# LM tower on one core: the first 16 score tiles of batch 0 straight from the projected rows

## The reference

```python
base = base_embeddings[ids]; rule = token_rules[ids]
h = einsum('bsd,bsde->bse', base, rule_transform[rule])        # one 64x64 matrix per token
xn = layernorm(h)
q = einsum('btd,hrd->bhtr', xn, Q); k = einsum('bud,hrd->bhur', xn, K)
attn = softmax(einsum('bhtr,bhur->bhtu', q, k) / sqrt(64))
h = h + einsum('bhtd,hde->bte', einsum('bhtu,bud->bhtd', attn, xn), VO)
x2 = layernorm(h)
gate = x2 @ Wg + bg + bias; w = softmax of the top 2, else 0
h = h + sum over e of w[e] * (relu(x2 @ W1[e] + b1[e]) @ W2[e] + b2[e])
```

## Time and profile before

| | us |
|---|---|
| median of 3 runs | 615.68 |
| lowest, highest | 615.65, 620.51 |
| profiled execution | 619.58 |
| its span, first to last instruction | 617.5 |
| mean granted TensorE clock | 0.923 of full |

### The profile page before, as it was taken

The page is one execution under the profiler, slowest core; times in us unless marked ns, Lnnn a source line. Parts: engine busy times, 40 slices in busy tenths (PEclk is TensorE's granted clock), DMA queues, the critical chain, the costliest instruction groups (busy, mean ns, idle before and its releaser), DMA issues.

```text
span 617.5 us, 9436 instructions
## 1 busy us (share of the span) xinstructions
PE 499.3 (81%) x2732; PEld 268.7 (44%) x2732; DVE 410.7 (67%) x1003; ACT 287.2 (47%) x581; POOL 228.3 (37%) x375
## 2 busy tenths in 40 slices
PE   0066603778679896999999999999999989999985
PEld 0035501234444342445544544454454444575753
DVE  5532486645215874978869877895975776665577
ACT  0203301025545543456564565556456546547664
POOL 5664356463225300340254145122413313181542
PEclk9998755559979997999999999999999999999989
DMA  8815212733381062440440422044042200000000
GB/s 234 312 59 152 79 36 61 179 95 103 95 229 40 14 155 53 102 113 5 100 114 2 102 63 60 1 104 113 1 96 68 53 2 2 11 2 10 11 2 17
DMA packets 21791, 47.05 MB, mean 76 GB/s; under 512 B 6248, under 2 KB 11576, under 8 KB 21680
## 3 DMA queue, kind: packets, MB, share of 16 engines
q1 hardware_dynamic: 15408, 32.23, 21.5%
q0 software_dynamic: 4752, 8.20, 4.9%
q10 hardware_dynamic: 1584, 6.03, 3.0%
HBM read 9.97 MB, written 11.01 MB: 34 GB/s over the span
## 4 chain that ended last, share of the span: by engine, by line
PE 54%; DVE 19%; issue 8%; DMA 6%; POOL 6%; ACT 3%; SPq 3%; another core or an unknown queue 0%; DVEq 0%; ACTq 0%; POOLq 0%
PE bank L1274 14%; PE bank L1260 10%; PE bank L1240 7%; PE bank L1202 4%; PE bank L1224 4%; DVE mx L997 3%; POOL emb_sorted L527 2%; DMA ctxT<-in_table,ids 2%; PE bank L1196 2%; PE bank L1197 2%; DVE r_sb L1055 2%; POOL ctxT L517 2%; PE bank L1132 2%; POOL r_sb L591 2%; DMA ks<-qk_l 1%
## 5 line engine op out<-in xcount | busy, mean ns | idle before, releaser
L997 DVE TENSOR_REDUCE mx<-bank 128x1 f32<-128x512 f32 x256 | 170.5, 687 | 83.5 <-PE bank L1260 75.3
L591 POOL TENSOR_TENSOR r_sb<-r_sb 128x256 f32<-128x256 f32 x174 | 91.0, 523 | 251.8 <-DVE r_sb L1073 171.4
L671 ACT ACTIVATE prob<-bank 128x512 f32<-128x512 f32 x256 | 139.0, 597 | 58.5 <-PE bank L1240 43.0
L1260 PE MATMUL bank<-ks,qs 96*128 96x512 f32 x256 | 122.7, 487 | 14.4 <-DVE mx L997 9.7
L1274 PE MATMUL bank<-prob,xa 128*64 128x512 f32 x448 | 123.5, 630 | 0.7 <-ACT ctxT L685 0.7
L1260 PEld LDWEIGHTS bank<-ks,qs 96*128 96x128 f32 x256 | 50.9, 199 | 130.8 <-issue 109.5
L1240 PE MATMUL bank<-qs,ks 97*128 97x512 f32 x224 | 78.1, 430 | 0.0
L738 ACT ACTIVATE r_sb<-bank,stay 128x512 f32<-128x512 f32 x56 | 37.1, 687 | 44.9 <-PE bank L1197 44.6
L1240 PEld LDWEIGHTS bank<-qs,ks 97*128 97x128 f32 x224 | 38.4, 194 | 15.6 <-issue 11.1
L527 POOL DMA_INDIRECT emb_sorted<-ctxT,pos x32 | 32.0, 1001 | 22.6 <-DMA emb_sorted<-ctxT,pos 11.7
L517 POOL DMA_INDIRECT ctxT<-in_table,ids x32 | 32.4, 1011 | 21.3 <-DMA ctxT<-in_table,ids 8.6
(11 more groups left out here) (167 smaller groups left out, 659.3 us busy)
## 6 DMA issues: line engine op xcount, KB each, us to landing
qs<-qk_h SPq DMA_DIRECT2D x64, 128.0 KB
ks<-qk_h SPq DMA_DIRECT2D x56, 128.0 KB
qs<-qk_l SPq DMA_DIRECT2D x32, 128.0 KB
ks<-qk_l SPq DMA_DIRECT2D x28, 128.0 KB
emb_sorted<-front ACTq DMA_DIRECT2D x4, 608.0 KB
y_sorted<-y_out POOLq DMA_DIRECT2D x19, 128.0 KB, 2.7
e_in<-emb_sorted POOLq DMA_DIRECT2D x9, 256.0 KB, 3.2
emb_sorted<-front ACTq DMA_DIRECT2D x3, 640.0 KB
```

Of the source, the lines that this page charges most:

```text
L591: nc.gpsimd.tensor_tensor(a[:, at:at + width], src[:, 0:width], src[:, width:2 * width], ALU.add).then_inc(S["pool_chain"], 1)
L671: nc.scalar.activation(prob[:, step % NPROB, u % 2, :], bank[u % NST][:], ACT.Exp, scale=SC).then_inc(S["exp_done"], 1)
L997: V.tensor_reduce(mx[:, u // 16, u % 16:u % 16 + 1], bank[3 + n % 2][:], AX.X, ALU.max).then_inc(S["mx_done"], 1)
L1260: M(bank[3 + n % 2][:], qs[0:96, nb % 2, h, tt * 128:(tt + 1) * 128], ks[0:96, nb % 2, h, :], start=True, stop=True).then_inc(S["s_ps"], 1)
```

## The change

In the first 16 places of batch 0's 32 score tiles PE computes pairs of tiles, one of a head of stack group g = 0 and one of g = 1 (rows 0 to 31 and 32 to 63), right from qk_h and qk_l: three matmuls of 32 rows a tile, high x high, low x high, high x low, summed in a bank, the two heads' matmuls in turn. Pairs take banks 3, 4 and 0, 1 alternately. A step still has two tiles; both are issued in the place of the first. mx keeps its columns. mt(0, 0) moves from (-1, 13) to (-1, 11), norm(1) from (0, 0) to (-1, 12), xT(1) from (0, 2) to (-1, 15), proj(1) from (0, 2) and (0, 3) to (0, 0) and (0, 1), the rule entries from (-1, 14) to (0, 5) to four a step in (0, 3) to (0, 7), norm(2), xT(2) and norm(3) one step on, proj(2) all to (0, 15), `bring(0, 1)` to right behind `bring(0, 0)`. `slots` is a generator, run for (1, 3) in five pieces at (-2, 1), (-2, 2), (-2, 5), (-2, 6) and (-2, 7). Norm pieces: 4 a step in b = -1, 3 in b = 0.

```diff
@@ -243,15 +243,15 @@
                     + [("back", f, 0), ("back", f, 1), ("fold", f, J), ("fold", f, J + 1)] + [("down", f + 1, p) for p in range(NE // 2)]
                     + [("back", f, 2), ("fold", f, J + 2), ("back", f, 3), ("fold", f, J + 3)])
 
-        R_AT = [(-1, 14), (-1, 15)] + [(0, g // 3) for g in range(18)]
+        R_AT = [(0, 3 + g // 4) for g in range(20)]
 
         def x_at(nb):
 
-            return {1: (0, 2), 2: (0, 13)}.get(nb, (nb - 2, XT))
+            return {1: (-1, 15), 2: (0, 14)}.get(nb, (nb - 2, XT))
 
         def proj_at(nb):
 
-            return {1: ((0, 2), (0, 2), (0, 3), (0, 3)), 2: ((0, 14), (0, 14), (0, 15), (0, 15))}.get(
+            return {1: ((0, 0), (0, 0), (0, 1), (0, 1)), 2: ((0, 15), (0, 15), (0, 15), (0, 15))}.get(
                 nb, [(nb - 2, k) for k in PROJ])
 
         def aux_at(b, k):
@@ -275,7 +275,7 @@
                 todo.append(("rt", b - 1, 0))
             if k == GATE and 0 <= b - 2 < B:
                 todo.append(("gate", b - 2, 0))
-            if k == MT[0] and 0 <= b + 1 < B:
+            if (b, k) == (-1, 11) or k == MT[0] and 0 <= b < B - 1:
                 todo.append(("mt", b + 1, 0))
             if k in VO_STEPS and 0 <= b - 1 < B:
                 todo.append(("vo", b - 1, VO_STEPS.index(k)))
@@ -384,6 +384,11 @@
             return ctxT[:, (LAST - 1) % 2].rearrange("p q t -> p (q t)").rearrange("p (e n) -> p e n", n=HW)
 
         NST = 3
+
+        def score_bank(n):
+
+            return bank[(3 if n >= 16 or n // 2 % 2 == 0 else 0) + n % 2]
+
         es = [t.rearrange("(g p s) d -> p g (s d)", p=128, s=4) for t in emb_sorted]
         ys = [t.rearrange("(g p s) d -> g p (s d)", p=128, s=4) for t in y_sorted]
 
@@ -554,6 +559,7 @@
             for g in range(NG[0] - 4, NG[0]):
                 store_sent(pool, g)
             bring(0, 0)
+            bring(0, 1)
             pool.wait_ge(S["zeroed_1"], 16 * 4)
             place(1, range(FIRST, FIRST + 2 * QC))
             values(0)
@@ -564,8 +570,6 @@
                     if n >= NE_IN // 2:
                         pool.wait_ge(S["eT_ps"], PAIRS[n - NE_IN // 2][-1] + 1)
                     load_pair(pool, n)
-                if n == NP0 + 2:
-                    bring(0, 1)
                 for g in PAIRS[n - AHEAD] if n >= NP0 + AHEAD else ():
                     pool.wait_ge(S["y_ok"], g + 1)
                     store_group(pool, g)
@@ -824,15 +828,19 @@
                 lo = SPAN[i][0]
                 both, nth, ahead, at_in, past, gap, tile_, hi, mid, low, two = (slot_i[:, j, :] for j in range(11))
                 link(V.tensor_tensor(sel[:], oh[:, c0 - lo:c1 - lo, :], key.unsqueeze(1).to_broadcast([128, QC, NR]), ALU.mult))
+                yield
                 link(V.tensor_reduce(slot_f[:], sel[:], AX.X, ALU.add))
+                yield
                 link(V.tensor_tensor(both, slot_f[:], rank[:, c0:c1], ALU.add))
                 link(V.tensor_scalar(nth, both, SHIFT, (B * T >> SHIFT) - 1, ALU.logical_shift_right, ALU.bitwise_and))
                 link(V.tensor_scalar(ahead, both, (B * T).bit_length() - 1, None, ALU.logical_shift_right))
                 link(V.tensor_scalar(at_in, both, TS - 1, 2, ALU.bitwise_and, ALU.logical_shift_left))
+                yield
                 link(V.tensor_tensor(past, nth, ahead, ALU.add))
                 link(V.scalar_tensor_tensor(gap, past, float(NR - 1), rule_i[:, c0:c1], ALU.add, ALU.subtract))
                 link(V.scalar_tensor_tensor(past, nth, 1.0, gap, ALU.min, ALU.mult))
                 link(V.tensor_tensor(tile_, past, rule_i[:, c0:c1], ALU.add))
+                yield
                 link(V.tensor_scalar(hi, tile_, 2, None, ALU.logical_shift_right))
                 link(V.tensor_scalar(low, tile_, 3, None, ALU.bitwise_and))
                 link(V.tensor_scalar(mid, hi, float(NG[i]), float(NG[i] * 512 + 256), ALU.is_lt, ALU.mult))
@@ -856,7 +864,7 @@
 
             run(look(0, 0))
             starts(0)
-            slots(0, 0)
+            run(slots(0, 0))
             tile_rules(0)
             run(look(1, 1))
             dve.wait_ge(S["w_h"], 3)
@@ -878,8 +886,8 @@
                     next(later, None)
             run(later)
             starts(1)
-            slots(1, 1)
-            slots(1, 2)
+            run(slots(1, 1))
+            run(slots(1, 2))
 
             def layernorm(b, done):
 
@@ -972,19 +980,22 @@
 
             gating = iter(())
             norms = []
-            N_AT = {1: (0, 0), 2: (0, 10), 3: (0, 14)}
+            N_AT = {1: (-1, 12), 2: (0, 11), 3: (0, 15)}
             for b in range(-2, B + 1):
                 if b == -2:
                     run(layernorm(0, "xn_ready"))
+                    later = slots(1, 3)
                 for k in range(16):
 
                     if (b, k) == (-2, 9):
-                        slots(1, 3)
+                        run(later)
                         tile_rules(1)
+                    if b == -2 and k in (1, 2, 5, 6, 7, 8):
+                        next(later, None)
                     if k == 0 and 0 <= b - 2 < LAST - 1:
                         norms.append(layernorm(b - 2, "xn2_ready"))
                     norms += [layernorm(nb, "xn_ready") for nb in range(1, B) if N_AT.get(nb, (nb - 3, 8)) == (b, k)]
-                    for _ in range((4 if k < 3 else 2) if b == 0 else 3 if b == LAST else 1):
+                    for _ in range(4 if b == -1 else 3 if b == 0 else 3 if b == LAST else 1):
                         while norms and next(norms[0], norms) is norms:
                             norms.pop(0)
                     if k == 0 and b < B or k in (9, 10, 11, 12) and b < LAST:
@@ -994,7 +1005,8 @@
                         dve.wait_ge(S["s_ps"], n + 1)
                         if nb >= 1 and u % 16 == 0:
                             dve.wait_ge(S["mt_ps"], 2 * nb - 1 + u // 16)
-                        V.tensor_reduce(mx[:, u // 16, u % 16:u % 16 + 1], bank[3 + n % 2][:], AX.X, ALU.max).then_inc(S["mx_done"], 1)
+                        at_ = u % 16 if n >= 16 else n % 2 * 8 + n // 2
+                        V.tensor_reduce(mx[:, u // 16, at_:at_ + 1], score_bank(n)[:], AX.X, ALU.max).then_inc(S["mx_done"], 1)
                     for a in aux_at(b, k):
                         kind, ab, i = a
                         if kind == "xT":
@@ -1225,6 +1237,20 @@
                                  vo_blk[:, pair, :, :].rearrange("p t e -> p (t e)"), start=True, stop=True)
                     last.then_inc(S["vo_ps"], 1)
 
+            def first_pair(n):
+
+                pe.wait_ge(S["qk_lo"], 4)
+                if n >= 4:
+                    pe.wait_ge(S["mx_done"], n - 2)
+                o, tt = n // 8, n // 2 % 4
+                for r, (q_, k_) in enumerate(((qk_h, qk_h), (qk_l, qk_h), (qk_h, qk_l))):
+                    for g in range(2):
+                        rows = slice(32 * g, 32 * g + 32)
+                        last = M(score_bank(n + g)[:], q_[rows, o, tt * 128:(tt + 1) * 128], k_[rows, 2 + o, :],
+                                 start=r == 0, stop=r == 2)
+                        if r == 2:
+                            last.then_inc(S["s_ps"], 1)
+
             for b in range(-2, B + 1):
                 for k in range(16):
                     step = 16 * b + k + 1
@@ -1253,6 +1279,10 @@
                             return
                         nb, u = todo.pop(0)
                         n = 32 * nb + u
+                        if n < 16:
+                            first_pair(n)
+                            todo.pop(0)
+                            return
                         h, tt = u // J, u % J
                         pe.wait_ge(S[f"stack_{h // 2}"], 96 * (nb + 1))
                         if n >= 2:
```

## The result

The changed kernel takes 612.23 us (median of 19 runs, 608.28 to 619.95); the kernel before, run beside it on the same chips, 619.02 (19 runs). The ratio is 0.9888, 95% interval [0.9863, 0.9913]: 6.9 us less, the interval 5.4 to 8.5. The forecast was 609.0 us, 6.7 less than the 615.68 that three executions before had given. In the profiled executions the span falls from 617.5 to 608.8, and the granted clock goes from 0.923 to 0.930. The profiled execution of the changed kernel (610.80 us) is 1.4 under its median and the one before (619.58) 0.6 over, so the rows show 2 us more than the medians do.

The account below looks back on a forecast made before the run. The later kernel was taken as a PE stream, so bringing it forward shortens all. Earlier starts, less what batch 2's rows give back, move the last qk_l from 217.5 to 210.8: 615.7 - 6.7 = 609.0 us, range 603 to 619.

Parts of the forecast that it names:

- slots in pieces, direct tiles behind qk_lo alone: Batch 0's projection: fourth projection 0.75 later, 5 us of slots behind it gone, PE free for direct tiles at 105.8.
- A pair at 1.28 on PE: Direct tiles: the two heads' matmuls run side by side, so a pair costs 3 x 0.43 = 1.28 us at half clock.
- the serial rival: Direct pairs run one after the other at half clock, 2.56 us each; total 618.2, slower; chance 0.08.
- drain: Direct tiles: the skill says a change of tiling mode drains TensorE; no profile row priced it.
- A pair every 1.3 us: Direct tiles: DVE's two reduces set the pace, 1.3 us a pair instead of 1.64; 16th reduce ends at 117.9.
- norm(1) early, (-1, 15) 5.5 us earlier: norm(1) in (-1, 12) and (-1, 13) lets (-1, 15) start at 126.3 instead of 131.85.
- bring(0, 1) ahead of the scatters, loads at 133.4: POOL's queue: four gathers add 5.1 us, rule loads go at 133.4, in by 136.6; hidden, (0, 3) needs them at 140.
- Rival 3: POOL's late scatters hold the first rules: loads land at 142.5, some 4 us lost, total 613; chance 0.1.
- (-1, 15) to (0, 3) in 13.9 us: Steps with xT(1), proj(1), no rules: 2.2 + 5.1 + 3.3 + 2.2 + 1.1 for the clock; (0, 3) at 140.2.
- Five rule steps at 8.4, 42.0: Steps (0, 3) to (0, 7), four rule entries each: 42.0 us, so (0, 8) starts at 182.2 instead of 192.37.
- Rival 1: Clock falls in the rule steps, 2.6 us a step: two steps 614.2, all five 622; chance 0.2.
- Batch 2's rows, 9.8 us from the last apply; DVE waits 3: Before norm(2): rows arrive at 191.6, its place comes at 188.5, DVE waits 3 us; last qk_l at 210.8.

Follow-up runs that it names:

- schedule_only: The changed kernel without direct tiles: the first 16 tiles come from the stacks again, all moved entries stay moved; ratio to the kernel before 0.9955.
- three_pairs: The changed kernel with three pairs of banks instead of two for the direct tiles; ratio to the kernel before 0.9858.
- bring_late: The changed kernel with bring(0, 1) back in its old place, behind three loads of phase 1; ratio to the kernel before 1.0192.
- rules_early: The changed kernel with the 20 rule entries five a step in (0, 2) to (0, 5); ratio to the kernel before 0.9883.
- pairs_norm_rules: The changed kernel with three bank pairs, norm(2) at (0, 12) and rule entries four a step from (0, 2) on; ratio to the kernel before 0.9800.
- norm_later: The changed kernel with norm(2) at (0, 12) instead of (0, 11); ratio to the kernel before 0.9884.
- slots_whole: The changed kernel with slots(1, 3) in one piece at (-2, 9), as before; ratio to the kernel before 0.9965.
- serial_heads: The changed kernel issuing one head's three matmuls of a direct pair, then the other's; ratio to the kernel before 0.9917.
- same_rows: The changed kernel with both tiles of a direct pair from one head, so on the same 32 rows; ratio to the kernel before 0.9927.
- pairs_norm: The changed kernel with three bank pairs for the direct tiles and norm(2) at (0, 12); ratio to the kernel before 0.9821.

## Why the prediction was right

The mechanism and the sum held: 6.7 us less was forecast, 6.9 measured (5.4 to 8.5). In the profiled pair the last qk_l moved by 7.8 us and the span by 8.7. Point by point, with the sizes that were off:

- *slots in pieces, direct tiles behind qk_lo alone.* Right, 0.5 late at the first tile (106.28 for 105.8), which is the later start of norm(0). What I had not said: without the direct tiles the stack's transfer would have held PE for 4.94 us (schedule_only). The two edits share one gain.
- *A pair at 1.28 on PE.* Right; the serial rival fell, and no drain shows: the first pair stands 0.51 behind the rule row. *A pair every 1.3 us* was mis-sized: "four banks let PE work a pair ahead" left out that a bank pair holds PE's 1.65 and DVE's 1.29 one after the other. It is 1.545, 1.4 us more over the sixteen tiles; three_pairs took it away. The gain of the direct tiles is thus their earlier start and not their pace, to which the sum had given 1.9 us (12.1 from the first score matmul to the 16th maximum, against 14.0; it is 13.5 against 13.6).
- *norm(1) early, (-1, 15) 5.5 us earlier.* Measured 3.8, the two terms above; counted from norm(0), 4.4.
- *bring(0, 1) ahead of the scatters, loads at 133.4.* Measured 133.76, with no wait at (0, 3). Rival 3 stayed away: POOL's groups waited 4.07, 3.78 and 1.45 us for the one before. The price of not moving it (17 to 18 us, bring_late) stood nowhere in the text.
- *(-1, 15) to (0, 3) in 13.9 us.* It took 10.8: the clock rose inside (0, 0), at some 130.5, a step before I had it rise. -3.1 us.
- *Five rule steps at 8.4, 42.0.* They took 40.1: the first was 6.4, with three applies in it, the others 7.8 to 9.0. The clock stayed full. Rival 1 didn't come in the changed kernel, but it did in neighbours: rules_early (0.52 from 150 to 160), pairs_norm_rules (0.71), and norm_later and slots_whole (0.66 from 160 to 170). That it stayed away was in part luck: norm_later differs from the changed kernel only in steps behind these.
- *Batch 2's rows, 9.8 us from the last apply; DVE waits 3.* 10.8 and 3.4. Then 19.8 to the last qk_l, 19.2 forecast. What the text lacked is the clock behind that wait: PE stood 3.9 us, and the window 190 to 200 reads 0.66. In serial_heads and same_rows the clock was down longer (0.50 from 190 to 200, and from 195 to 205), and both took 32.4 us from (0, 8) to the last qk_l, the changed kernel 30.7.

The errors are of both signs (+0.5, +1.4, -3.1, -1.9, +1.0, +0.6; they add to -1.5, and with what is left between the steps the last qk_l is 1.1 early), and the near hit of the total owes something to that. So does the 6.9 itself: the profiled pair shows 2 us more than the medians, and one profile of each can't say how the medians' difference divides over the steps.

## What to carry to other kernels

When an edit makes an early stage faster, list everything that the stage's successor waits for, and move all of it: here the tiles alone cost 0.8%, their schedule alone gave 0.5%, and both gave 1.1%. Ask what a faster stage spares: here it was a wait for a transfer and not the stage's own time. Between two engines that hand banks to and fro, the pace is their two times added and divided by the number of bank sets, if that is longer than the slower engine's own. A wait of several microseconds on TensorE costs more than its length where the clock falls behind it. A norm that starts late enough to find its rows spared some of that in two runs (1.0 us up to the last qk_l in norm_later, more in pairs_norm with the third bank pair), though no ratio shows that move by itself.

## What the runs showed of the hardware that was not expected

- Matmuls on rows 0 to 31 and 32 to 63 overlap whatever the order in the queue: in serial_heads the second head's first matmul, fourth in the queue, started with the first one (103.17, x2). The Trainium skill ("TensorE: Matmul & The Clock Gate", Part 3: Packing small matmuls) says that such matmuls run concurrently, and there the trace agrees; it also says that their starts keep the program's order, and there the trace differs: had they, the rows would read three of one head and then three of the other.
- Six matmuls of 32 rows and 512 columns of two heads: 1.28 us a pair at half clock; of one head they follow one another at 0.43, with the neighbouring pair in between (3.94 for two pairs). How far ahead a matmul on other rows may start showed in the first pairs of same_rows, where no bank held it: the seventh in the queue started at 107.60, with the third (107.59), and not with the first (106.57).
- The clock fell behind PE waits of 2.9 to 3.9 us in front of norm(2) (changed, serial_heads, same_rows, three_pairs), where the pv matmuls (L1304) right behind took 1.98 us for four. They took 1.08 behind 0.74 and 1.80 in pairs_norm and behind 0.79 in norm_later, and 1.27 there behind 2.35. The length of the last wait alone doesn't decide it: in rules_early they took 1.98 behind 0.95, and in pairs_norm_rules 1.98 behind 1.98.
